# Moving one unit's input product from GpSimd to VectorE in the recurrent stage of a four-layer kernel

## The chip, the cores and the metric

The kernel runs on one core of a Trainium2 chip. A core has TensorE (matrix products, into PSUM), VectorE, ScalarE and GpSimd (elementwise work; GpSimd does not touch PSUM here), and SyncE, whose queue issues transfers. The engines run their own instruction streams and meet at semaphores. The metric is the device time of one execution in microseconds; the kernel before takes 3253.26 us (median of 3 runs, 3252.29 to 3256.7).

## The reference

Four layers one after the other on 16 sequences of 128 rows and 512 columns: an attention layer with an MLP, a grouped attention layer, a recurrent layer, and a latent attention layer with an MLP. Only the recurrent one matters here. Per sequence (l rows, h = 32 heads of s_ = 16):

```python
xm = xa[:, :, None] + sx[:, :, None] * (maa_stack + xxx)      # five mixed row sets k, w, v, r, g
w = jnp.exp(-jnp.exp(time_decay + jnp.tanh(xw @ td_w1) @ td_w2)).reshape(b, l, h, s_)
r = (xr @ Wr.T).reshape(b, l, h, s_)
k = (xk @ Wk.T).reshape(b, l, h, s_)
v = (xv @ Wv.T).reshape(b, l, h, s_)
def step(s, rkvw):
    r_t, k_t, v_t, w_t = rkvw
    a = k_t[..., :, None] * v_t[..., None, :]
    out = jnp.einsum('bhi,bhij->bhj', r_t, u * a + s)
    s = a + w_t[..., :, None] * s
    return (s, out)
```

The state s is 16 x 16 per head. The outputs are normalised per head, gated, projected and added to the input (x1); then a small gated MLP with shifted rows follows.

## The kernel before, in words

`recurrence_phase` (L2564) is the recurrent stage. A sequence's states are cut into 8 units (`UNITS`, `NU = 8`): 4 groups of 128 state rows `m` times 2 halves `jh` of the value index, in the order jh = 0 with m = 0 to 3, then jh = 1 with m = 0 to 3. The unit with index u = 4 is the fifth, (m = 0, jh = 1). Each unit has a tile of 128 x 8 x 128 values, one of four `S` buffers (`S[u % 4]`), and passes through:

1. `inputs(s, u)`: the outer product k x v for all 128 times, written to S from column 1 on. On VectorE (L3134) it reads `vb[jh]` (values copied to all partitions by SyncE's DMA, `load_v`) and the keys straight from PSUM (`k_bank`). On GpSimd (L2829) it reads `vb[jh]` and a copy of the keys in SBUF (`k_sb`), which ScalarE makes (`keys_copy`, L2988). `ON_POOL = [2, C]`, with C = 4, says which units GpSimd forms: the third and the fifth.
2. ScalarE puts the first state into column 0 (`first_states`, L2892).
3. `scan(s, u)` on VectorE (L3149): the recurrence over time, in place.
4. `multiply_states(s, u)` on GpSimd (L2818): times the receptance r, in place.
5. `sum_heads(s, u)` on TensorE (L3454): the sum over the state index, into `rec_out`. The semaphore `reduced` then frees the S buffer.

The units are interleaved by hand with the work of other sequences. `run_steps` calls each engine's `step(ahead, front, middle, back, tail)`: a step does the recurrence of one sequence (middle), the projections of the next (front), the first normalisation of the one after (ahead), the head normalisation, output projection and start of the MLP of the previous one (back), and the end of the MLP of the one before (tail). The first and last steps are written out with constants in the waits, and lack some of these parts; the steps between run in a hardware loop of two steps a turn with counts from registers.

VectorE's order in a step around the change is: `scan(middle, 3)`, `mix(front, 3)` (L3112 product, L3120 sum), `residual(back)` (L3211, which waits for the output rows `o` of TensorE, then the row statistics L3089 to L3094), `output(tail)` (L3229, L3231), `scan(middle, 4)`, `mix(front, 4)`, `stats_front(ahead)`, `inputs` and `scan` of unit 5, `inputs` of unit 6, `mix_back(back, 0)` (L3221, which waits for ScalarE's shifted rows L2940), `scan(middle, 6)`.

GpSimd's order there is: `multiply_states` of unit 3, the input product of unit 4, the back sequence's reciprocal root (`rsqrt`, L2809, L2810, L2812), `multiply_states` of unit 4, the ahead sequence's `rsqrt`, `multiply_states` of units 5 and 6.

TensorE's order there is: the transpose `rstd_t` (L3476), head sums of unit 1, the v projection, output rows 0 and 1 (L3344), head sums of unit 2, two mix products, output rows 2 and 3, and so on; the transposed back rows `normed_t` (L3331) come behind the head sums of unit 4.

The count `NA = NU - len(ON_POOL)` is the number of VectorE's input products per sequence. SyncE's `load_states` and `load_v`, and TensorE's `keys`, wait for counts of them (`a_done`).

Of the kernel before, what the change touches and what calls it, by code (L numbers as in the profile page):

```python
# [24 lines left out]
C = D // 128  # L25
# [25 lines left out]
def wait_count(engine, sem, count):  # L51

    if not isinstance(count, int) or count > 0:
        engine.wait_ge(sem, count)
# [178 lines left out]
def bcast(ap, shape, axis):  # L233
    return ap.unsqueeze(axis).to_broadcast(shape)
# [2329 lines left out]
def recurrence_phase(nc, cfg, const, x_in, x_out, ctx, state_t, weights, own_weights, next_weights):  # L2564
# [13 lines left out]
    NU = len(UNITS)  # L2578
    ROOT = 9

    ON_POOL = [2, C]
    NA = NU - len(ON_POOL)
    SETUP = 7

    with ExitStack() as stack:
        def sb(n, shape, dt=F32):
            return stack.enter_context(nc.sbuf_tensor(f"rec_{n}", shape, dt))
# [22 lines left out]
        rk = sb("rk", [128, C, T])  # L2610
        k_sb = sb("k_sb", [128, len(ON_POOL), T])
        c_sb = sb("c_sb", [128, T])
# [190 lines left out]
        def _(pool):  # L2803
# [18 lines left out]
            def inputs(s, n):  # L2822

                u = ON_POOL[n]
                m, jh = UNITS[u]
                pool.wait_ge(vb_loaded[jh], s.n * 16 + 16)
                pool.wait_ge(k_copied, s.n + 1)
                wait_count(pool, reduced, s.n * NU + u - 3)
                nc.gpsimd.tensor_tensor(S[u % 4][:, :, 1:T], vb[jh][:, :, 0:T - 1],  # L2829
                                        bcast(k_sb[:, n, 0:T - 1], [128, JH, T - 1], 1), ALU.mult)\  # L2830
                    .then_inc(pool_a_done, 1)
# [19 lines left out]
            def step(ahead, front, middle, back, tail):  # L2851
                if back:
                    multiply_states(back, NU - 1)
                if middle:
                    multiply_states(middle, 0)
                    inputs(middle, 0)
                if middle:
                    multiply_states(middle, 1)
                if back:
                    first_columns(back)  # L2860
                if middle:
                    bonus_values(middle)
                    multiply_states(middle, 2)
                if middle:
                    multiply_states(middle, 3)
                    inputs(middle, 1)
                if back:
                    rsqrt(back.n, stats2, rstd2, back_norm[2], rstd2_done)
                if middle:
                    multiply_states(middle, 4)  # L2870
                if ahead and not is_first(ahead.n):
                    rsqrt(ahead.n - 1, stats, rstd, front_norm[2], rstd_done)
                if middle:
                    multiply_states(middle, 5)
                    multiply_states(middle, 6)
# [7 lines left out]
        def _(act):  # L2883
# [99 lines left out]
            def keys_copy(s):  # L2983
                act.wait_ge(k_full, s.n + 1)
                wait_count(act, pool_a_done, s.n * len(ON_POOL))
                for n, u in enumerate(ON_POOL):
                    m = UNITS[u][0]
# [97 lines left out]
        def _(dve):  # L3085
# [42 lines left out]
            def inputs(s, u):  # L3128
                m, jh = UNITS[u]
                dve.wait_ge(vb_loaded[jh], s.n * 16 + 16)  # L3130
                if u == 0:
                    dve.wait_ge(k_full, s.n + 1)
                wait_count(dve, reduced, s.n * NU + u - 3)
                nc.vector.tensor_tensor(S[u % 4][:, :, 1:T], vb[jh][:, :, 0:T - 1],  # L3134
                                        bcast(k_bank[s.k][:, m * T:m * T + T - 1], [128, JH, T - 1], 1), ALU.mult)\
                    .then_inc(a_done, 1)

            def scan(s, u):
                m, jh = UNITS[u]
                St = S[u % 4]  # L3140
                if u in ON_POOL:
                    dve.wait_ge(pool_a_done, s.n * len(ON_POOL) + ON_POOL.index(u) + 1)
                else:
                    dve.wait_ge(a_done, s.n * NA + [v for v in range(NU) if v not in ON_POOL].index(u) + 1)
                dve.wait_ge(s0_done, s.n * NU + u + 1)
                if jh == 0:
                    dve.wait_ge(decay_done, s.n * C + m + 1)
                flat = "p j t -> p (j t)"
                nc.vector.tensor_tensor_scan(St[:, :, :].rearrange(flat), decay[m][:, :, :].rearrange(flat),  # L3149
                                             St[:, :, :].rearrange(flat), 0.0,  # L3150
                                             ALU.mult, ALU.add).then_inc(scan_done, 1)
# [82 lines left out]
            def step(ahead, front, middle, back, tail):  # L3234
                if middle:
                    inputs(middle, 0)
                    scan(middle, 0)
                if back:
                    gather(back)
                if front:  # L3240
                    mix(front, 1)
                if middle:
                    inputs(middle, 1)
                if back:
                    head_centre(back)
                if front:
                    mix(front, 2)
                if middle:
                    scan(middle, 1)
                if back:  # L3250
                    head_rsqrt(back)
                    head_norm(back)
                if middle:
                    scan(middle, 2)
                if front:
                    mix(front, 0)
                if back:
                    gated(back)
                if middle:
                    inputs(middle, 3)  # L3260
                    scan(middle, 3)
                if front:
                    mix(front, 3)
                if back:
                    residual(back)
                if tail:
                    output(tail)
                if middle:
                    scan(middle, 4)
                if front:  # L3270
                    mix(front, 4)
                if ahead and not is_first(ahead.n):
                    stats_front(ahead)
                if middle:
                    inputs(middle, 5)
                    scan(middle, 5)
                    inputs(middle, 6)
                if back:
                    mix_back(back, 0)
                if middle:  # L3280
                    scan(middle, 6)
                if back:
                    mix_back(back, 1)
                if front:
                    make_gate(front)
                if middle:
                    inputs(middle, 7)
                    scan(middle, 7)
                if ahead:
                    shift_front(ahead)  # L3290
                if front:
                    bonus_products(front)
# [552 lines left out]
```

## Time and profile before

| | value |
|---|---|
| median of 3 runs | 3253.26 us |
| profiled execution | 3253.45 us |
| its span, first to last instruction | 3251.7 us |
| TensorE busy | 3020.7 us (93%) |
| VectorE busy | 2049.7 us (63%) |
| GpSimd busy | 1259.9 us (39%) |
| ScalarE busy | 1243.0 us (38%) |
| mean granted TensorE clock | 0.976 |

The profile is of one execution. "Busy" is summed over the whole kernel, so each share is a mean over stages with different limits; the rows of the recurrent stage have to be read apart. Times in timelines are microseconds from the span's start. Releasers of waits are inferred from semaphore events.

### The profile page before, as it was taken

To read this page: it belongs to the slowest core of one execution; us is meant where nothing else is said; L and a number is where in the kernel's file an instruction comes from. 1 tells how busy PE (TensorE), PEld (TensorE's weight loads), DVE (VectorE), ACT (ScalarE), POOL (GpSimd) and SP (SyncE) were. 2 spreads that over 40 slices of the span, in tenths; PEclk is the share of its full clock that TensorE was granted. 3 is DMA by queue.
4 is the path that set the end of the run, shared out by engine and by line. 5 is a ranking of instruction groups with operands and counts; after the bars stand their busy time and mean duration, and the time that the engine had idled before them with its cause. 6 is when DMAs were issued, how large, how long until landed. Compare 5 with 4: busy or idle time off the path is not lost. (4 is left out here: it accounts for less than half of the span.)

```text
span 3251.7 us, 58799 instructions
## 1 busy us (share of the span) xinstructions
PE 3020.7 (93%) x21184; PEld 2197.2 (68%) x21184; DVE 2049.7 (63%) x3098; ACT 1243.0 (38%) x4419; POOL 1259.9 (39%) x899
## 2 busy tenths in 40 slices
PE   7999799989999889987899999997799999899999
PEld 5666566669999756655676677675455545499998
DVE  4665455564544468885899999998254454564543
ACT  2444344442322357762343443442243333332322
POOL 3555355551000045663566666666033223330000
PEclk9999899999999899998999999998899999999999
DMA  4111141110000231111111111111130011011010
GB/s 166 54 42 34 53 159 55 49 40 27 13 26 26 75 146 55 55 42 63 47 41 43 49 53 36 42 50 30 66 144 28 33 34 37 33 41 39 19 39 14
DMA packets 104318, 170.31 MB, mean 52 GB/s; under 512 B 16512, under 2 KB 54016, under 8 KB 100736
## 3 DMA queue, kind: packets, MB, share of 16 engines
q1 hardware_dynamic: 99296, 124.58, 12.0%
q10 hardware_dynamic: 4896, 44.04, 3.4%
q8 instruction: 80, 1.31, 0.2%
q14 instruction: 46, 0.38, 0.0%
HBM read 135.03 MB, written 33.55 MB: 52 GB/s over the span
## 5 line engine op out<-in xcount | busy, mean ns | idle before, releaser
L2818 POOL TENSOR_TENSOR rec_S<-rec_S,rec_r_t 128x1024 f32<-128x1024 f32 x128 | 306.1, 2392 | 255.9 <-DVE rec_S L3149 254.6
L3149 DVE TENSOR_TENSOR_SCAN rec_S<-rec_decay,rec_S 128x1024 f32<-128x1024 f32 x128 | 303.6, 2373 | 8.9 <-DVE rec_S L3134 2.1
L581 POOL TENSOR_TENSOR latent_scores<-latent_scores,region_a 128x1024 f32<-128x1024 f32 x64 | 119.9, 1895 | 390.8 <-DVE region_a L881 390.1
L1607 ACT ACTIVATE group_scores<-group_scores,group_negmax 128x128 f32<-128x128 f32 x512 | 197.6, 391 | 33.7 <-DVE group_negmax L1716 23.9
L1556 POOL TENSOR_TENSOR group_scores<-group_scores,group_rowsum 128x512 f32<-128x512 f32 x128 | 130.6, 1050 | 176.9 <-DVE group_rowsum L1730 176.9
L671 ACT ACTIVATE latent_scores<-latent_scores,region_a 128x256 f32<-128x256 f32 x256 | 126.4, 498 | 67.7 <-DVE region_a L858 67.7
L671 ACT ACTIVATE cross_scores<-cross_scores,cross_negmax 128x128 f32<-128x128 f32 x256 | 98.8, 390 | 78.0 <-DVE cross_negmax L858 77.9
L671 ACT ACTIVATE self_scores<-self_scores,self_negmax 128x128 f32<-128x128 f32 x256 | 98.7, 389 | 78.0 <-DVE self_negmax L858 77.9
L2216 ACT ACTIVATE mlp_h_t<-mlp_h_t,vectors 128x128 f32<-128x128 f32 x256 | 81.3, 390 | 114.5 <-DVE mlp_h_t L2311 92.1
L2216 ACT ACTIVATE pmlp_h_t<-pmlp_h_t,vectors 128x128 f32<-128x128 f32 x256 | 81.3, 390 | 113.5 <-DVE pmlp_h_t L2311 91.1
L3454 PE MATMUL rec_rec_out<-rec_S,head_sum 128*32 128x256 f32 x1024 | 84.1, 401 | 43.1 <-POOL rec_S L2818 42.0
L3134 DVE TENSOR_TENSOR rec_S<-rec_vb,rec_k 128x1016 f32<-128x1016 f32 x96 | 115.2, 1200 | 0.0
L1067 PE MATMUL latent_pjA<-latent_src_t,F_query_key 128*128 128x512 f32 x240 | 114.4, 600 | 0.0
L567 POOL TENSOR_TENSOR cross_scores<-cross_scores,cross_bias 128x1024 f32<-128x1024 f32 x32 | 75.1, 2358 | 77.9 <-DVE cross_scores L847 77.4
L567 POOL TENSOR_TENSOR self_scores<-self_scores,self_bias 128x1024 f32<-128x1024 f32 x32 | 75.0, 2357 | 69.3 <-DVE self_scores L847 68.8
L1607 ACT ACTIVATION_READ_ACCUMULATOR group_scores<-group_scores,group_negmax 128x1 f32 x512 | 97.9, 191 | 0.0
L868 DVE COPY region_a<-latent_pjP 128x512 f32<-128x512 f32 x48 | 32.7, 681 | 102.7 <-PE latent_pjP L1132 102.7
L581 POOL TENSOR_TENSOR cross_scores<-cross_scores,cross_rinv 128x512 f32<-128x512 f32 x64 | 68.0, 1078 | 73.0 <-DVE cross_rinv L881 73.0
L581 POOL TENSOR_TENSOR self_scores<-self_scores,self_rinv 128x512 f32<-128x512 f32 x64 | 68.0, 1079 | 72.2 <-DVE self_rinv L881 72.2
L2418 PE MATMUL pmlp_bank<-pmlp_src_t,region_a 128*128 128x128 f32 x768 | 92.7, 278 | 0.8 <-ACT pmlp_src_t L2204 0.8
L2418 PE MATMUL mlp_bank<-mlp_src_t,region_a 128*128 128x128 f32 x768 | 91.1, 275 | 1.2 <-ACT mlp_src_t L2204 1.2
L2418 PEld LDWEIGHTS pmlp_bank<-pmlp_src_t,region_a 128*128 128x128 f32 x768 | 90.5, 195 | 1.4 <-ACT pmlp_src_t L2204 1.0
(475 smaller groups left out, 7942.7 us busy)
## 6 DMA issues: line engine op xcount, KB each, us to landing
rec_vb<-v_by_head SPq DMA_DIRECT2D x32, 512.0 KB, 4.3
region_a<-in_C_w ACTq DMA_DIRECT2D x2, 4096.0 KB, 20.0
region_a<-in_G_w ACTq DMA_DIRECT2D x2, 4096.0 KB, 19.1
self_xres<-in_x SPq DMA_DIRECT2D x16, 256.0 KB, 2.7
cross_ctx_t<-in_ctx_t SPq DMA_DIRECT2D x16, 256.0 KB, 3.4
cross_xres<-rows_A SPq DMA_DIRECT2D x16, 256.0 KB, 2.6
mlp_x<-rows_B SPq DMA_DIRECT2D x16, 256.0 KB, 2.8
group_ctx_t<-in_ctx_t SPq DMA_DIRECT2D x16, 256.0 KB, 3.2
```

What stands on the lines that cost most here:

```text
L567: nc.gpsimd.tensor_tensor(half, half, bias[:, u, :].unsqueeze(1).unsqueeze(1).to_broadcast([128, 4, 2, T]), ALU.add).then_inc(bias_added, 1)
L581: nc.gpsimd.tensor_tensor(heads, heads, inverse, ALU.mult).then_inc(probs_scaled, 1)
L671: nc.scalar.activation(S[:, u, at, :], S[:, u, at, :], ACT.Exp, bias=negmax[:, u, at.start // KB:at.start // KB + 1], accum_out=rowsum[:, ...
L1067: last = nc.tensor.matmul(pj.bank(item)[:, :], Wk[:, c, n * 128:n * 128 + 128], src_t[:, c, :, :], start=c == 0, stop=c == C - 1)
L1556: nc.gpsimd.tensor_tensor(heads, heads, bcast(rowsum[:, u, 4 * r:4 * r + 4], [128, 4, T], 2), ALU.mult).then_inc(probs_scaled, 1)
L1607: nc.scalar.activation(S[:, u, at, :], S[:, u, at, :], ACT.Exp, bias=negmax[:, u, at:at + 1], accum_out=rowsum[:, u, j:j + 1])\
L2216: last = nc.scalar.activation(tile[:, n, :], tile[:, n, :], ACT.Gelu_apprx_tanh, bias=vec(cfg["b1"], half * HB + n))
L2418: last = nc.tensor.matmul(M[n][:, i * T:(i + 1) * T], w[:, c, f:f + 128], rows[:, c, :], start=c == 0, stop=c == 1)
L2818: nc.gpsimd.tensor_tensor(S[u % 4][:, :, :], S[u % 4][:, :, :], bcast(r_t[:, s.k, UNITS[u][0], :], [128, JH, T], 1), ALU.mult)\
L3134: nc.vector.tensor_tensor(S[u % 4][:, :, 1:T], vb[jh][:, :, 0:T - 1], bcast(k_bank[s.k][:, m * T:m * T + T - 1], [128, JH, T - 1], 1), ALU ...
L3149: nc.vector.tensor_tensor_scan(St[:, :, :].rearrange(flat), decay[m][:, :, :].rearrange(flat), St[:, :, :].rearrange(flat), 0.0, ALU.mult, ...
L3454: last = nc.tensor.matmul(rec_out[32 * g:32 * g + 32, jh * 2 * T:(jh + 1) * 2 * T], head_sum, S[u % 4][:, 2 * g:2 * g + 2, :], start=m == ...
```

## The change

GpSimd forms the inputs of the third unit only. VectorE forms those of the fifth too, right behind the scan of the fourth, in the S buffer that the first unit has left.

```diff
@@ -2578,7 +2578,7 @@
     NU = len(UNITS)
     ROOT = 9
 
-    ON_POOL = [2, C]
+    ON_POOL = [2]
     NA = NU - len(ON_POOL)
     SETUP = 7
 
@@ -2863,7 +2863,6 @@
                     multiply_states(middle, 2)
                 if middle:
                     multiply_states(middle, 3)
-                    inputs(middle, 1)
                 if back:
                     rsqrt(back.n, stats2, rstd2, back_norm[2], rstd2_done)
                 if middle:
@@ -3259,6 +3258,7 @@
                 if middle:
                     inputs(middle, 3)
                     scan(middle, 3)
+                    inputs(middle, 4)
                 if front:
                     mix(front, 3)
                 if back:
```

With `ON_POOL` one shorter, NA goes from 6 to 7, `keys_copy` copies one group of keys instead of two, and the waits for `pool_a_done` count one per sequence instead of two.

## Rows read from the trace of the kernel before

**Rows 1.** Stretches of the recurrent stage: us, each engine's busy time (x instructions), clock, DMA.
```profile
1523.00:2280.00 757.00, 696.08 (x5380) 508.48 (x5380) 694.38 (x922) 292.40 (x764) 486.91 (x310) 0.97 0.14 42
...
1735.63:1783.23 47.60, 45.92 (x360) 33.66 (x359) 44.43 (x61) 19.59 (x51) 30.73 (x21) 1.00 0.14 45
1783.23:1830.65 47.42, 45.51 (x356) 33.24 (x356) 44.43 (x61) 19.60 (x51) 30.57 (x21) 1.00 0.14 45
```

**Rows 2.** Timeline of TensorE: start, duration, instruction, [idle before <- releaser].
```profile
1819.79 0.33 PE L3476 MATMUL rec_bank_n<-ident,rec_hy 128*128 128x128 f32 x1 [0.46 <-DVE rec_hy L3191]
...
1828.63 1.98 PE L3344 MATMUL rec_bank_c<-region_a,rec_og_t 128*128 128x512 f32 x4
```

**Rows 3.** Timeline of VectorE in the same sequence.
```profile
1829.53 0.69 DVE L3120 TENSOR_TENSOR rec_xm<-rec_bank_b,rec_xa_t 128x512 f32<-128x512 f32 x1
1830.65 0.69 DVE L3211 TENSOR_TENSOR rec_x<-rec_bank_c,rec_xr 128x512 f32<-128x512 f32 x1 [0.43 <-PE rec_bank_c L3344]
...
1833.30 0.69 DVE L3231 SCALAR_TENSOR_TENSOR rec_y<-rec_bank_d,rec_x 128x512 f32<-128x512 f32 x1
1833.91 2.28 DVE L3149 TENSOR_TENSOR_SCAN rec_S<-rec_decay,rec_S 128x1024 f32<-128x1024 f32 x1
...
1839.91 2.29 DVE L3149 TENSOR_TENSOR_SCAN rec_S<-rec_decay,rec_S 128x1024 f32<-128x1024 f32 x1
...
1843.35 1.13 DVE L3221 SCALAR_TENSOR_TENSOR rec_f_in<-rec_bank_c,rec_w_same,rec_f_in 128x128 f32<-128x128 f32 x4
```

**Rows 4.** Timeline of ScalarE in the same sequence.
```profile
1840.44 2.88 ACT L2940 ACTIVATE rec_f_in<-rec_bank_c,vectors,rec_w_shift 128x127 f32<-128x127 f32 x8
```

**Rows 5.** Timeline of GpSimd in the same sequence.
```profile
1831.14 2.35 POOL L2829 TENSOR_TENSOR rec_S<-rec_vb,rec_k_sb 128x1016 f32<-128x1016 f32 x1
...
1834.21 1.96 POOL L2812 TENSOR_TENSOR rec_rstd<-rec_rstd 128x1 f32<-128x1 f32 x1
1836.27 2.36 POOL L2818 TENSOR_TENSOR rec_S<-rec_S,rec_r_t 128x1024 f32<-128x1024 f32 x1
...
1839.49 0.20 POOL L2812 TENSOR_TENSOR rec_rstd<-rec_rstd 128x1 f32<-128x1 f32 x1
```

**Rows 6.** The S tile's instructions: count, duration in ns (min/median/max), first and last start.
```profile
L3134 DVE TENSOR_TENSOR rec_S<-rec_vb,rec_k x96: 1181/1201/1214, 1521.9 to 2273.6; 128x1016 f32<-128x1016 f32 x96
L2829 POOL TENSOR_TENSOR rec_S<-rec_vb,rec_k_sb x32: 2343/2358/2376, 1527.8 to 2256.6; 128x1016 f32<-128x1016 f32 x32
```

**Rows 7.** Timeline of VectorE, first step (first two rows) and the loop (third).
```profile
1526.89 1.20 DVE L3134 TENSOR_TENSOR rec_S<-rec_vb,rec_k 128x1016 f32<-128x1016 f32 x1
1528.01 0.69 DVE L3112 TENSOR_TENSOR rec_bank_a<-rec_bank_a,rec_sx_t 128x512 f32<-128x512 f32 x1
...
1807.06 2.29 DVE L3149 TENSOR_TENSOR_SCAN rec_S<-rec_decay,rec_S 128x1024 f32<-128x1024 f32 x1 [0.21 <-DVE rec_S L3134]
```

**Rows 8.** Timeline of VectorE, the residual one step later.
```profile
1878.25 0.69 DVE L3211 TENSOR_TENSOR rec_x<-rec_bank_c,rec_xr 128x512 f32<-128x512 f32 x1 [0.64 <-PE rec_bank_c L3344]
```

**Rows 9.** Timeline of VectorE in the first, the second and the last step.
```profile
1545.00 0.70 DVE L3112 TENSOR_TENSOR rec_bank_b<-rec_bank_b,rec_sx_t 128x512 f32<-128x512 f32 x1 [4.96 <-PE rec_bank_b L3380]
...
1546.84 2.29 DVE L3149 TENSOR_TENSOR_SCAN rec_S<-rec_decay,rec_S 128x1024 f32<-128x1024 f32 x1 [0.34 <-POOL rec_S L2829]
...
1590.73 0.70 DVE L3112 TENSOR_TENSOR rec_bank_b<-rec_bank_b,rec_sx_t 128x512 f32<-128x512 f32 x1 [1.29 <-PE rec_bank_b L3380]
...
1606.32 1.12 DVE L3221 SCALAR_TENSOR_TENSOR rec_f_in<-rec_bank_c,rec_w_same,rec_f_in 128x128 f32<-128x128 f32 x4 [2.55 <-ACT rec_f_in L2940]
...
2254.70 0.69 DVE L3211 TENSOR_TENSOR rec_x<-rec_bank_c,rec_xr 128x512 f32<-128x512 f32 x1 [0.50 <-PE rec_bank_c L3344]
...
2258.96 2.29 DVE L3149 TENSOR_TENSOR_SCAN rec_S<-rec_decay,rec_S 128x1024 f32<-128x1024 f32 x1 [1.03 <-POOL rec_S L2829]
```

**Rows 10.** Timeline of GpSimd in the second and the last step.
```profile
1600.55 2.10 POOL L2812 TENSOR_TENSOR rec_rstd<-rec_rstd 128x1 f32<-128x1 f32 x1
...
2261.82 2.35 POOL L2818 TENSOR_TENSOR rec_S<-rec_S,rec_r_t 128x1024 f32<-128x1024 f32 x1
```

## The prediction

> **What bounds the kernel now.** I read the stretches first: the recurrent stage runs from 1523 to 2280 us, 757 us of the span [rows 1]. It handles 16 sequences; from the third on one takes 47.4 or 47.6 us in turn, with VectorE busy 44.4 us and TensorE 45.5 to 45.9 us of it, GpSimd 30.6. So two engines have little room and GpSimd has much. Which of the two sets the time changes within a sequence, and the timelines say where. From the transpose at 1819.79 TensorE runs without a gap to the output rows, whose last product starts at 1828.63 and ends at 1830.61 [rows 2]. VectorE has finished the mix for row set 3 at 1829.53 + 0.69 = 1830.22 and stands still for 0.43 us until those rows come [rows 3]. Up to there TensorE is late, by 0.43 us. From the residual (1830.65) to the scan of the fifth unit (1833.91), the sixth (1839.91), and the products at 1843.35, VectorE runs on back to back [rows 3]; ScalarE's shifted rows, ending at 1840.44 + 2.88 = 1843.32, arrive just then and themselves follow from the same fifth scan over GpSimd [rows 4]. That second half is VectorE's, and what delays the fifth scan delays the sequence.
>
> GpSimd's work on a state and VectorE's scan do not run beside each other: the last small GpSimd operation of the back sequence starts at 1834.21, inside the scan of 1833.91 to 1836.19, and lasts 1.96 us, ending at 1836.17, where it otherwise takes 0.20 [rows 5]. The input-forming product on VectorE reads one operand from PSUM, and next to a running GpSimd multiply it keeps its 1.20 us: the range over all 96 is 1181 to 1214 ns [rows 6].
>
> The Trainium skill (GPSIMD Engine Reference, Specifications) says that GpSimd shares its SBUF interfaces with VectorE and contends where VectorE's instruction has two SBUF inputs. By that the added product, with one, costs no lock, and the scans do; the rows agree.
>
> **The change, part by part.**
> *Removed on GpSimd:* 16 products of 2.36 us [rows 6], at 1831.14 in the sequence shown [rows 5]. Its end, 1833.49, lies 0.42 us before VectorE comes to the fifth scan (1833.91), so in the loop no one waits for it: worth nothing on the path. Behind it GpSimd now takes up the back sequence's root when the variance is there, about 1833.2, and ends it some 1.0 us later, ahead of the scan, rather than in it. Its reader on ScalarE is then early by nearly 2 us, but TensorE transposes those rows only behind the fifth unit's head sums, and these wait for the multiply that starts at the scan's end (1836.27, 0.08 after it) [rows 5]. No gain.
>
> *Added on VectorE:* 16 products of 1.20 us [rows 6]. What counts is what one takes from start to start of the next. Nothing in the loop shows it ahead of a mix product; in the first step such a pair starts 1.12 us apart (1526.89, 1528.01) [rows 7], and that is the lower bound. Ahead of a scan that depends on it the scan stands idle another 0.21 us (at 1807.06), which makes 1.41, the upper one [rows 7]. I take 1.15, near the like pair. Its waits are met before: the first unit's head sums, last readers of its buffer, stand in TensorE's order well ahead of the transpose of 1819.79, and the value rows of the second half and the keys are there since the step began. Queued behind it are the mix for row set 3, the residual and the output, then the fifth scan.
>
> *What idle time takes it up:* the wait for the output rows, 0.43 us in one step and 0.64 in the next [rows 3, 8]. Back-to-back starts also overlap by 0.08 (the scan at 1833.91 starts before 1833.30 + 0.69 = 1833.99) [rows 3]. Of the 13 steps whose sequence is the third to the fifteenth, 5 show 0.64 and 8 show 0.43: 6.6 us of waits, and 13 x 0.08 = 1.0 of overlap. Steps 3 to 15 cost 13 x 1.15 - 7.6 = 7.3 us, 0.6 or 0.4 us each. The next engine late there is VectorE itself.
>
> *The ends of the stage.* In the first step VectorE idles 4.96 us ahead of the mix for row set 3, so the product is free there, and the fifth scan no longer waits 0.34 us for GpSimd's input [rows 9]; with the overlap that is -0.4. In the second step it idles 1.29 us there, which hides the 1.15: 0. In the last step (no front sequence) the residual waits 0.50 us for TensorE and the fifth scan 1.03 us for GpSimd's input [rows 9]. The product takes 1.12 there (constant waits, as in the first step), of which the 0.50 and 0.08 of overlap hide a part: the residual starts 0.55 late. The fifth scan, without its 1.03 and with 0.08 of overlap, starts 1.03 + 0.08 - 0.55 = 0.56 early. Its multiply came only at 2261.82, 0.57 behind the scan's end (2258.96 + 2.29 = 2261.25), for the root in front of it ran into the scan [rows 9, 10]. That root is now done before the scan, so the multiply follows at 0.08 and gains 0.56 + 0.49, and with it the rest: -1.05.
>
> *Everything else:* the ScalarE key copy loses one of its two 0.2 us pieces and one wait; ScalarE has over 27 us idle per sequence [rows 1], so 0. The SP queue waits for the count of VectorE's products at the unit of index 3 and at the last one; both counts grow with NA and name the same instruction as before, so loads issue where they did. The second value load goes out behind the last product of the sequence before, most of a step ahead of its new first reader. If it did come late there, all of VectorE's queue would stand behind it; as GpSimd read the same buffer at 1831.14, some 2 us later than VectorE now does, with no wait before it, I cost it at nothing.
>
> *Sum:* -0.4 + 0 + 7.3 - 1.05 = +5.8 us on the profiled execution's 3253.45 (span 3251.7 and 1.75 around it; 0.2 us above the median of the runs), 3259.3. With the bounds 1.12 and 1.41 for the product: +5.5 and +9.3, 3258.9 and 3262.7. If a product costs its full 1.20 and no idle time gives way: 13 x 1.20 - 1.45 = +14.2, 3267.6.
>
> A measurement of this kernel tells a difference from none at about 0.2%, 6.5 us. The forecast lies just inside.
>
> **The rivals.**
> *A root caught by the sixth scan (slower).* For the following sequence GpSimd computes a root between the fifth multiply and the sixth scan. In the loop its last operation starts at 1839.49 and the scan at 1839.91: 0.42 us of room [rows 3, 5]. In the second step that operation started at 1600.55, inside the sixth scan, and took 2.10 us; VectorE then waited 2.55 us for ScalarE's shifted rows (1606.32) [rows 9, 10]. If the change upset the order so in every loop step, each would cost 2.5 us more: 12 x 2.5 + 5.8 = +36, 3289. It decides at a multiply more than 0.42 us late behind the fifth scan. Against it: the back root now starts 1.3 us before the scan and needs 1.0, so it frees GpSimd sooner. 0.07.
>
> *GpSimd's relief counts in each step (faster).* If the fifth scan waited for GpSimd's input in the loop too, as it does in the last step, each step would gain that 1.05: 13 x -1.05 - 1.45 = -15, 3238. Against it: the scan shows no idle ahead of it in any loop step, and 0.42 us of room. 0.08. A rule points the same way: the Trainium skill (GPSIMD Engine Reference, Engine selection) wants elementwise work on a tile on VectorE, GpSimd being about twice as slow with two inputs. The rows agree on the rate (2.36 against 1.20), and by durations alone the change would save 16 x 1.16 = 18.6 us. Rates say nothing of which engine is waited for, and here it is the one that gets the work.
>
> *The product disappears in waits (no change).* Scans behind their inputs show up to 0.21 us of idle in the loop [rows 7], and the overlaps and waits around the transposes are of the same size. If two such gaps took up another 0.4 us per step: 5.8 - 13 x 0.4 = +0.6, 3254. All of them lie in parts that move as a whole, so 0.09.
>
> *The change doesn't do what it says.* The product is issued before a mix instead of right ahead of its scan; should VectorE's own order make it wait for the head sums of the first unit, those come before the transpose of 1819.79. No separate chance.
>
> **How the numbers follow.** Forecast 0.72, of which 0.42 lies below +6.5 us and 0.30 above (the bounds +5.5 to +9.3, and unrecovered idle up to +14). Root caught 0.07, relief 0.08, no change 0.09, and 0.04 left, split evenly over slower and same. Slower 0.30 + 0.07 + 0.02 = 0.39; same 0.42 + 0.09 + 0.02 = 0.53; faster 0.08. The range goes from 3253 (the no-change case taken in) to 3267 (idle time that gives nothing); it leaves out both collisions, some 0.2 in all with the forecast's own tails. The forecast's own range is 3257 to 3263.
>
> **What would show it.** Right: VectorE has 112 products of L3134's kind and GpSimd 16; the idle of 0.43 or 0.64 ahead of the residual (L3211) is gone; the loop's sequences take about 48.0 us each, no longer in turn; the small root operation (L2812) of the back sequence lasts 0.2 and not 2 us; the fifth scan of the last sequence has no wait. Wrong if the idle is still there (then TensorE's rows moved too), if a product lasts more than 1.25 us, if L3221 shows new waits for ScalarE, or if the sequence still takes 47.5.

## The result and the profile after

The changed kernel took 3261.15 us, the kernel before 3253.74 us in runs beside it (medians of 11): a ratio of 1.0021, with a 95% interval of 1.0012 to 1.0030. That is 7.4 us more between the medians, and 3.9 to 9.8 by the interval. The forecast was 3259.3 us, +5.8. The profiled execution of after took 3259.06 us, with a span of 3257.3 us, 5.6 us longer than before's 3251.7.

First the busy times of the whole span, from the page of after, and then the stretch of the recurrent stage (columns as in [rows 1]).

```profile
PE 3018.7 (93%) x21184; PEld 2195.3 (67%) x21184; DVE 2066.4 (63%) x3114; ACT 1241.9 (38%) x4403; POOL 1197.1 (37%) x883
```
```profile
1522.50:2280.00 757.50, 694.51 (x5369) 506.81 (x5367) 710.12 (x937) 290.78 (x748) 421.20 (x291) 0.97 0.14 42
```

Against [rows 1], VectorE is busy 710.1 us where it was 694.4, GpSimd 421.2 where it was 486.9. The first difference, 15.7 us (16.7 in the totals of the two pages), is less than 16 products of 1.20 us (19.2): a product overlaps its neighbours, and busy time counts the overlap once. The second, 66 us, is more than the 16 products of 2.36 us (38 us); the rest is mostly small GpSimd operations that no longer stand in a scan. The S tile's instructions in after (count; ns min, median, max) confirm the exchange, one for one, with unchanged durations [rows 6]:

```profile
L3133 DVE TENSOR_TENSOR rec_S<-rec_vb,rec_k x112: 1178/1202/1215, 1521.1 to 2277.0; 128x1016 f32<-128x1016 f32 x112
L2829 POOL TENSOR_TENSOR rec_S<-rec_vb,rec_k_sb x16: 2340/2362/2373, 1527.1 to 2242.4; 128x1016 f32<-128x1016 f32 x16
```

The timeline of VectorE in after, one step past that of [rows 3] (a step with a wait of 0.64 before, [rows 8]):

```profile
1874.84 2.46 DVE L3148 TENSOR_TENSOR_SCAN rec_S<-rec_decay,rec_S 128x1024 f32<-128x1024 f32 x1 [0.21 <-ACT rec_S L2891]
1877.22 1.18 DVE L3133 TENSOR_TENSOR rec_S<-rec_vb,rec_k 128x1016 f32<-128x1016 f32 x1
1878.32 0.69 DVE L3111 TENSOR_TENSOR rec_bank_b<-rec_bank_b,rec_sx_t 128x512 f32<-128x512 f32 x1
1879.11 0.69 DVE L3119 TENSOR_TENSOR rec_xm<-rec_bank_b,rec_xa_t 128x512 f32<-128x512 f32 x1
1879.72 0.68 DVE L3210 TENSOR_TENSOR rec_x<-rec_bank_c,rec_xr 128x512 f32<-128x512 f32 x1
```

The added product stands between the fourth scan and the mix, and the residual behind them (L3210 now) has no wait. From the fourth scan's start to the mix's start it is 3.48 us. In before it was 2.44:

```profile
1826.29 2.46 DVE L3149 TENSOR_TENSOR_SCAN rec_S<-rec_decay,rec_S 128x1024 f32<-128x1024 f32 x1 [0.21 <-ACT rec_S L2892]
1828.73 0.70 DVE L3112 TENSOR_TENSOR rec_bank_b<-rec_bank_b,rec_sx_t 128x512 f32<-128x512 f32 x1
```

So the product adds 1.04 us to VectorE's queue, for a duration of 1.18. From its own start to the mix's it is 1.10 us (1877.22 to 1878.32), and it starts 2.38 us behind the scan, 0.06 sooner than the mix did. Behind the mix the residual now starts after 1.40 us (1878.32 to 1879.72), where it took 1.92 us in before with the wait of 0.43 and 2.13 with the wait of 0.64. So 0.52 or 0.73 us of the 1.04 are taken up there.

GpSimd in the step of [rows 5], in after:

```profile
1834.54 0.19 POOL L2812 TENSOR_TENSOR rec_rstd<-rec_rstd 128x1 f32<-128x1 f32 x1
1837.43 2.36 POOL L2818 TENSOR_TENSOR rec_S<-rec_S,rec_r_t 128x1024 f32<-128x1024 f32 x1 [2.69 <-DVE rec_S L3148]
1840.65 0.19 POOL L2812 TENSOR_TENSOR rec_rstd<-rec_rstd 128x1 f32<-128x1 f32 x1
```

The last operation of the back sequence's root ends 0.34 us before the fifth scan starts (1835.07 in after) and lasts 0.19 us, not 1.96. The following sequence's root (1840.65) is still ahead of the sixth scan (1841.06).

All marks of the stage, as a table. Each is counted from the stage's first scan, and the columns are what the kernel adds to before's mark. They are read from the timelines of VectorE.

| mark | before, us | after | after_again |
|---|---|---|---|
| residual of step 2 | 69.56 | -0.16 | -0.78 |
| residual of step 15 | 687.30 | +5.16 | +4.45 |
| last unit's head sums read | 757.32 | +4.17 | +3.80 |
| next stage's first instruction | 797.36 | +6.30 | +5.20 |

So the thirteen steps from the third to the fifteenth cost 5.3 us (5.2 in the second profile), the last step gives 1.0 (0.65) back, and the drain behind it is 2.1 (1.4) us longer, although the change touches nothing there. The stage of after begins 0.7 us earlier than before's, and 6.3 - 0.7 is the 5.6 us between the spans. In after_again the stage begins 1.65 us later than before's, so of the 7.8 us between those spans only 5.2 are the stage's own.

### The profile page after: what moved, and what is told of

It reads as the page before. It is cut to its first block and busy times, and to the rows that moved or that the text cites. A ratio compares the mean times of both kernels' runs of the same rounds, so it can differ in the third digit from the quotient of the medians.

```text
span 3257.3 us, 58793 instructions
## 1 busy us (share of the span) xinstructions
PE 3018.7 (93%) x21184; PEld 2195.3 (67%) x21184; DVE 2066.4 (63%) x3114; ACT 1241.9 (38%) x4403; POOL 1197.1 (37%) x883
## 5 line engine op out<-in xcount | busy, mean ns | idle before, releaser
L3133 DVE TENSOR_TENSOR rec_S<-rec_vb,rec_k 128x1016 f32<-128x1016 f32 x112 | 134.2, 1198 | 0.0
L2418 PEld LDWEIGHTS mlp_bank<-mlp_src_t,region_a 128*128 128x128 f32 x768 | 90.2, 194 | 1.8 <-ACT mlp_src_t L2204 1.4
```

What stands on the lines that cost most here:

```text
L2418: last = nc.tensor.matmul(M[n][:, i * T:(i + 1) * T], w[:, c, f:f + 128], rows[:, c, :], start=c == 0, stop=c == 1)
```

## Experiments

No kernel below leaves out work. Two add some: "twice" forms the fifth product two times, "idle_pool" forms it once more into a buffer that nobody reads. Ratios are to the kernel before, run beside each. A loop step is the mean of twelve, from the residual of step 3 to that of step 15; before it is 47.46 us.

**The two kernels again.** Copies of after and before, timed in the same way.

> The changed kernel once more. My theory (VectorE is the late engine from the residual to the seventh scan, and the product costs what the idle ahead of the residual does not take up): loop steps of 47.9 us on average against 47.5, no idle ahead of the residual, and 3.4 to 3.5 us lost between the first scan of the stage and the last head sums' reader, as in the first profile of it, whatever the total. The 2.1 us that the first profile lost in the drain of the stage (output rows 6.65 us against 5.36) are then the granted clock's, and may be there or not. Rival (the drain is slower because of the change): the same 2 us in the same rows again. Total 3259 to 3262 either way.

> The kernel before, once more, for a second profile. Between the reader of the last head sums and the first instruction of the next stage the profiles so far show 40.0 us (before), 42.2 and 41.4 (after), 40.5 to 41.6 (three variants). If that drain depends on the phase of the granted clock only, this one may show anything between 40 and 42; if the change makes it longer, 40.0 again. Ratio 1.000 within its interval, loop steps of 47.46 us on average.

Measured: after_again 3260.89 us, ratio 1.0020 (1.0011 to 1.0029), loop step 47.86. before_again 3254.57 us, 1.0004 (0.9995 to 1.0013), loop step 47.46 and every mark within 0.02 us of before's. The difference of 0.2% is the change's, and a mark of the loop can be read to some hundredths. Marks of the first step and of the drain can't: two profiles of the same changed kernel differ there by 0.6 and 0.7 us.

**Twice the dose.** The product is formed a second time right ahead of itself.

```diff
                     scan(middle, 3)
+                    inputs(middle, 4, True)    # counts on a semaphore of its own, and waits for it
                     inputs(middle, 4)
```

> The changed kernel with the fifth unit's product formed twice by VectorE, the second behind a wait on the first (the same values twice). My theory: the idle ahead of the residual is used up by the first, so the second costs its full 1.2 plus 0.04 to 0.2 for the wait in each of steps 3 to 15, about 1.0 in the second, nothing in the first (3.8 us of idle left), 1.2 in the last: 14 to 18 + 2 = 16 to 20 us above the changed kernel, 3277 to 3281, loop steps of 49.1 to 49.3 us. Rival (VectorE's work is hidden beside TensorE's, and the loss of the change comes from somewhere else, for instance the earlier GpSimd root or the clock): less than 5 us above the changed kernel.

Measured: 3278.21 us, 1.0074 (1.0060 to 1.0087), loop step 49.12, which is 1.67 above before and 1.26 above after. VectorE's timeline in "twice" (the two products grouped):

```profile
1836.79 2.42 DVE L3134 TENSOR_TENSOR rec_S<-rec_vb,rec_k 128x1016 f32<-128x1016 f32 x2
1839.13 0.69 DVE L3112 TENSOR_TENSOR rec_bank_b<-rec_bank_b,rec_sx_t 128x512 f32<-128x512 f32 x1
```

The pair takes 2.34 us to the mix's start. The second dose costs 1.26 us in each step, the first 0.41: the first met idle time at the residual, the second none. (The wait for its own first product is part of the 1.26.)

**The same product behind the idle time.** It is formed right ahead of the fifth scan instead of behind the fourth.

```diff
                     scan(middle, 3)
-                    inputs(middle, 4)
...
+                    inputs(middle, 4)
                     scan(middle, 4)
```

> The changed kernel with the product moved from behind the fourth scan to right ahead of the fifth, behind the residual and the output: the same VectorE work. My theory: the idle of 0.43 or 0.64 us ahead of the residual is back and absorbs nothing, and the scan that depends on the product starts 0.04 to 0.2 behind it, so each loop step costs 1.2 to 1.4 more than before the change (48.7 to 48.9 us), the whole 3271 to 3275. Rival (only VectorE's sum of work counts, not where it stands): 3261, as the changed kernel.

Measured: 3270.19 us, 1.0050 (1.0036 to 1.0064), loop step 48.78, or 1.32 above before: the step as expected, the whole 1 us under the range given. VectorE's timeline in "late", and then what the idle time ahead of its residual waited for (us, times):

```profile
1833.66 0.69 DVE L3210 TENSOR_TENSOR rec_x<-rec_bank_c,rec_xr 128x512 f32<-128x512 f32 x1 [0.43 <-PE rec_bank_c L3344]
...
1836.92 1.20 DVE L3133 TENSOR_TENSOR rec_S<-rec_vb,rec_k 128x1016 f32<-128x1016 f32 x1
1838.25 2.29 DVE L3148 TENSOR_TENSOR_SCAN rec_S<-rec_decay,rec_S 128x1024 f32<-128x1024 f32 x1
```
```profile
  PE rec_bank_c L3344: 13.1, 16
```

In after the second view reads:

```profile
  PE rec_bank_c L3344: 7.3, 2
```

Of these, one wait in either kernel is that of the drain behind the last step (5.55 us in late, 6.83 in after), and the other one in after is that of step 2 (0.42).

In late the idle time of 0.43 us is back, and the product costs its full start-to-start time, 1.33 us ahead of the scan that reads it. It is the same product at the same duration: the place makes 0.9 us per step.

**Half and three quarters of it on VectorE.** From the kernel before: GpSimd forms only the other rows, VectorE forms its part behind the fourth scan, and the fifth scan waits for both.

```diff
# GpSimd, unit 4 only: the part from j0 on
+                j0 = 0 if n == 0 else JH // 2          # three_quarters: 3 * JH // 4
# VectorE, unit 4 only: the part up to j1
+                j1 = JH // 2 if u == C else JH         # three_quarters: 3 * JH // 4
```

> The fifth unit's product cut in halves: VectorE forms rows 0 to 3 of 8 behind the fourth scan, GpSimd rows 4 to 7 in its old place. My theory: VectorE's half takes about 0.6 us, which 0.43 or 0.64 us of idle and 0.1 of overlap cover, so a loop step costs 0 to 0.1 us more than before (47.5 us) and less than half of the change's 0.4; a dose curve with its bend between half and whole. In the last step the fifth scan waits no longer for GpSimd, -1.0. Total -1.0 to +0.5 us against before. Rival (the cost is in proportion to VectorE's work): half of the change's loss, loop steps of 47.66, +2 to +3.5 us.

> The split kernel with 6 of 8 rows of the fifth product on VectorE and 2 on GpSimd. My theory (idle first, then full price): VectorE's part takes 0.25 to 0.3 us longer from start to start than the half, which left nothing of the 0.43 idle and 0.2 of the 0.64: loop steps 0.25 and 0.05 us longer than before in turn, 47.6 on average; +1 to +2 us less 1.2 in the last step, so 3252 to 3256. In proportion to the work it would be 0.3 us in every step.

Measured: split 3253.07 us, 0.9999 (0.9990 to 1.0008), loop step 47.45. three_quarters 3256.30 us, 1.0008 (0.9999 to 1.0017), loop step 47.61. VectorE's timeline in "split":

```profile
1826.28 2.45 DVE L3151 TENSOR_TENSOR_SCAN rec_S<-rec_decay,rec_S 128x1024 f32<-128x1024 f32 x1 [0.21 <-ACT rec_S L2893]
1828.65 0.65 DVE L3136 TENSOR_TENSOR rec_S<-rec_vb,rec_k 128x508 f32<-128x508 f32 x1
1829.23 0.69 DVE L3113 TENSOR_TENSOR rec_bank_b<-rec_bank_b,rec_sx_t 128x512 f32<-128x512 f32 x1
...
1830.64 0.69 DVE L3213 TENSOR_TENSOR rec_x<-rec_bank_c,rec_xr 128x512 f32<-128x512 f32 x1
```

Half a product moves the mix from 2.44 to 2.95 us behind the fourth scan, so it adds 0.51 us. The residual starts 4.36 us behind that scan, just as in before (1826.29 to 1830.65). Against VectorE's share of the product, 0, 1/2, 3/4, 1 and 2, a loop step grows by 0.00, 0.00, 0.15, 0.41 and 1.67 us. The mix comes 0, 0.51, 0.78, 1.04 and 2.28 us later. Take from this the 0.52 or 0.73 us that the place ahead of the residual can give, and the mean over the steps is the measured growth to within 0.02 us. It is flat until the idle time is full, and then it rises by the full time of the work.

**What the GpSimd relief is worth in the loop.** After, with GpSimd kept about as busy as before by a product nobody reads (two halves, 2.63 us together where one whole product took 2.36).

```diff
                     multiply_states(middle, 3)
+                    spare_product(middle)      # two halves into a buffer that is free there
```

> The changed kernel, with GpSimd still doing a product of the old size in the old place (two halves into a tile that is unused then, read by no one), so only VectorE's side of the change is there. My theory: loop steps as in the changed kernel (47.9 us), since GpSimd's relief is worth nothing there; in the last step the back root runs into the fifth scan again and the scan itself may be held, so that 1 us of the end's gain is lost: 1 to 2 us above the changed kernel, 3262 to 3263. Rival (GpSimd's relief pays in every step and hides a larger VectorE loss): 0.4 to 1 us per step more, 3267 to 3276.

Measured: 3261.34 us, 1.0022 (1.0013 to 1.0031), loop step 47.90, against 47.87 in after. GpSimd's timeline in "idle_pool":

```profile
1830.53 2.63 POOL L2838 TENSOR_TENSOR rec_xn<-rec_vb,rec_k_sb 128x508 f32<-128x508 f32 x2
1833.88 2.21 POOL L2812 TENSOR_TENSOR rec_rstd<-rec_rstd 128x1 f32<-128x1 f32 x1
```

The back root is caught by the fifth scan again (issued while the scan runs, it ends with it): 2.21 us for an operation of 0.19, and the step is 0.03 us longer. In the loop the relief is worth nothing. At the end it is worth something: from the residual of step 15 to the last head sums after gains 1.0 us on before, and idle_pool loses 0.4 (+5.74 to +6.12).

**The last step alone.** From the kernel before: only in the last sequence does VectorE form that product.

```diff
-                    inputs(middle, 1)
+                    if not is_last(middle):
+                        inputs(middle, 1)
...
                     scan(middle, 3)
+                    if is_last(middle):
+                        inputs(middle, 4)
```

> The kernel before, with the last sequence's fifth product alone on VectorE. My theory: all loop steps as before; in the last step the fifth scan starts 0.5 us earlier than before, its multiply 1.0, and the reader of the last head sums comes 1.0 us sooner: -1.0 us in the profile from the first scan to that reader, too little for the timed runs. Rival (the last step's gain in the change's profile came from the steps before): 0.

Measured: 3254.36 us, 1.0003 (0.9994 to 1.0012). The residual of step 15 is at -0.09, the last head sums at -1.16: 1.07 us gained in the last step, of which 0.39 is left at the next stage's first instruction. VectorE's timeline in "last_only" (fifth and sixth scan of the last sequence):

```profile
2259.49 2.28 DVE L3152 TENSOR_TENSOR_SCAN rec_S<-rec_decay,rec_S 128x1024 f32<-128x1024 f32 x1
2262.91 3.44 DVE L3152 TENSOR_TENSOR_SCAN rec_S<-rec_decay,rec_S 128x1024 f32<-128x1024 f32 x1
```

The fifth scan waits no longer [rows 9]. The sixth, issued while a GpSimd multiply runs, lasts 3.44 us.

**GpSimd on the sixth unit instead.** After, and GpSimd forms the sixth unit's product behind its multiply for the fourth unit, VectorE no longer. VectorE then has as many products as before, and GpSimd too. The room between the following sequence's root and the sixth scan is what is at stake.

```diff
-    ON_POOL = [2]
+    ON_POOL = [2, 5]
...
                     multiply_states(middle, 3)
+                    inputs(middle, 1)
...
-                    inputs(middle, 5)
```

> The changed kernel with the sixth unit's product given to GpSimd in return (in the place where the fifth's was), so VectorE forms six of eight again: one more in the half where TensorE is late, one less in the half where VectorE is. By VectorE's work alone: 1.2 us less per loop step than the change, 0.8 less than before, 3243 to 3246. My theory: VectorE comes to the sixth scan 1.2 us earlier, just behind the fifth multiply, and the scan catches GpSimd's small root of the following sequence, whose last operation has 0.42 us of room; ScalarE's shifted rows then come about 2 us late behind it, VectorE waits for them at the back products, and a loop step takes 48.5 to 49.5 us: 3268 to 3282.

Measured: 3287.27 us, 1.0103 (1.0088 to 1.0119), loop step 50.09. GpSimd, ScalarE and VectorE in "sixth":

```profile
1897.60 2.23 POOL L2809 TENSOR_TENSOR rec_rstd<-rec_stats,rec_single 128x1 f32<-128x1 f32 x1
1900.40 0.19 POOL L2812 TENSOR_TENSOR rec_rstd<-rec_rstd 128x1 f32<-128x1 f32 x1
```
```profile
1900.63 0.81 ACT L2924 ACTIVATE rec_x<-rec_x,rec_rstd 128x512 f32<-128x512 f32 x1 [3.14 <-POOL rec_rstd L2812]
1901.35 2.87 ACT L2940 ACTIVATE rec_f_in<-rec_bank_c,vectors,rec_w_shift 128x127 f32<-128x127 f32 x8
```
```profile
1904.26 1.12 DVE L3221 SCALAR_TENSOR_TENSOR rec_f_in<-rec_bank_c,rec_w_same,rec_f_in 128x128 f32<-128x128 f32 x4 [3.31 <-ACT rec_f_in L2940]
```

This is the slower rival of the prediction, brought about on purpose. Forming the sixth product elsewhere brings the sixth scan nearer to the root. The scan catches the root's first small operation, not its last as I had expected; ScalarE has the normalisation that needs the root in its queue ahead of the shifted rows, and VectorE waits 3.31 us for those. The price was put at 1.0 to 2.0 us per step above before and was 2.6.

**The same, with ScalarE's order changed.** The shifted rows of the back sequence come ahead of the following sequence's normalisation.

```diff
-                if ahead and not is_first(ahead.n):
-                    normalise_front(ahead)
...
                     shifted_back(back)
+                if ahead and not is_first(ahead.n):
+                    normalise_front(ahead)
```

> The kernel of the run sixth (fifth product on VectorE, sixth on GpSimd), with two entries of ScalarE's order exchanged: the shifted rows come ahead of the following sequence's normalisation, so they no longer stand behind GpSimd's caught root. If the caught root is what cost the run sixth its 2.6 us per loop step, the wait of 3.31 us ahead of the back products falls to under 1, and a step takes 47.5 to 47.9 us (the seventh scan then waits for the multiply that the root delays): 3252 to 3260. If the cost is GpSimd's and the scans' contention as such, the step stays above 49 us.

Measured: 3253.64 us, 0.9999 (0.9990 to 1.0008), loop step 47.36. GpSimd and VectorE in "sixth_act":

```profile
1832.65 2.23 POOL L2809 TENSOR_TENSOR rec_rstd<-rec_stats,rec_single 128x1 f32<-128x1 f32 x1
```
```profile
1836.88 1.13 DVE L3221 SCALAR_TENSOR_TENSOR rec_f_in<-rec_bank_c,rec_w_same,rec_f_in 128x128 f32<-128x128 f32 x4 [0.87 <-ACT rec_f_in L2940]
```

The root is caught just as before, 2.23 us, but of the wait of 3.31 only 0.87 is left. So nearly all the harm came through ScalarE's queue. A smaller one stays: the multiply for the sixth unit starts 0.70 us behind the sixth scan's end, where it is 0.08 in after, and what that costs was not tried by itself.

**Two versions built on that.** "mix_last" takes sixth_act and lets VectorE form the sixth product in the last sequence only. "mix_last_pe" also exchanges two entries of TensorE's order.

```diff
# mix_last, on sixth_act
-                    inputs(middle, 1)
+                    if not is_last(middle):
+                        inputs(middle, 1)
...
+                    if is_last(middle):
+                        inputs(middle, 5)
# mix_last_pe, on mix_last, TensorE
-                if middle:
-                    sum_heads(middle, 4)
...
                     normed_t(back)
+                if middle:
+                    sum_heads(middle, 4)
```

> The kernel of the run sixth_act, with GpSimd left out of the last sequence's sixth product (VectorE forms it there too). In sixth_act the loop steps took 47.36 us against 47.46 before, and its first steps gained 3.8 us, but the last step lost 2.0 of that, where GpSimd's input ran in front of the roots. My theory: with the last step like that of the changed kernel it gains 1 instead, so the reader of the last head sums comes some 6 us sooner than before the change, of which the clock in the drain may give back 1 to 2: 3247 to 3251, a ratio of 0.998 to 0.999. Rival (the loss of the last step has nothing to do with GpSimd's product): 3 us slower than that, as sixth_act.

> mix_last with TensorE's transpose of the back rows ahead of the fifth unit's head sums. The shifted rows then come early and VectorE's wait for them (0.87 us in sixth_act's steps) goes. My theory: nothing is won, since the seventh scan starts when GpSimd's sixth multiply lets it, at the same time as now: loop steps of 47.3 to 47.4 us. Rival (that wait is on the path): 0.5 to 0.9 us less per loop step, 3236 to 3243.

Measured: mix_last 3249.87 us, 0.9984 (0.9975 to 0.9993), loop step 47.35. mix_last_pe 3243.93 us, 0.9965 (0.9951 to 0.9978), loop step 47.26: faster than both kernels of this case. mix_last gained the 3 us expected at the last head sums (-6.10, sixth_act -3.05). For mix_last_pe I had expected next to nothing, since the seventh scan can't work before GpSimd's multiply for the sixth unit has ended. That multiply starts 11.0 us behind the residual in both kernels. GpSimd and VectorE in the loop of mix_last_pe:

```profile
1838.39 2.37 POOL L2818 TENSOR_TENSOR rec_S<-rec_S,rec_r_t 128x1024 f32<-128x1024 f32 x1
```
```profile
1838.70 1.12 DVE L3224 SCALAR_TENSOR_TENSOR rec_f_in<-rec_bank_c,rec_w_same,rec_f_in 128x128 f32<-128x128 f32 x4
1839.74 3.17 DVE L3152 TENSOR_TENSOR_SCAN rec_S<-rec_decay,rec_S 128x1024 f32<-128x1024 f32 x1
```

The wait of 0.87 ahead of the products is gone, and a scan of 2.29 us, issued 1.02 us before the multiply ends, takes 3.17 instead. That is the exchange I had reckoned with, and a step gains 0.09 us by it. What I missed is the last two steps, where VectorE waits for the shifted rows, and the seventh scan behind them lasts only 0.25 us longer without the wait. In "mix_last" it waits there:

```profile
2221.25 1.13 DVE L3224 SCALAR_TENSOR_TENSOR rec_f_in<-rec_bank_c,rec_w_same,rec_f_in 128x128 f32<-128x128 f32 x4 [0.99 <-ACT rec_f_in L2941]
...
2267.12 1.13 DVE L3224 SCALAR_TENSOR_TENSOR rec_f_in<-rec_bank_c,rec_w_same,rec_f_in 128x128 f32<-128x128 f32 x4 [1.89 <-ACT rec_f_in L2941]
```

In mix_last_pe both waits are gone, and at the last head sums it stands at -10.23, 4.1 us ahead of mix_last; 1.4 us of that was there at step 15, the rest are these two waits, nearly whole. The remaining 2.2 us of the stage come in the drain (below), and are the granted clock's.

## Why the prediction came out right, point by point

**What bounds the step.** Right, and shown. TensorE, with the output rows, was late at the residual by 0.43 or 0.64 us, VectorE everywhere behind it. "late" shows that the idle time belongs to that place, "split" that it holds half a product for nothing, "twice" that what exceeds it costs its full time.

**The added product.** The step that reasoned from the pair of the first step was right in kind and a little high: 1.15 us was taken, with 1.12 as the lower bound. From start to start it is 1.10, and the product also starts sooner behind the scan than the mix did, so it adds 1.04. With that the thirteen steps would be 13 x 1.04 - 7.6 = +5.9; measured are +5.3, predicted were +7.3. Most of the other 0.6 us stands in two places. In the third, fourteenth and fifteenth step of before the mix itself had waited 0.08 us, and there the product adds only 0.95 (3.59 us for 2.64 from scan to mix). And at the residual 8 x 0.52 + 5 x 0.73 = 7.8 us are taken up, not 7.6. That gives 10 x 1.04 + 3 x 0.95 - 7.8 = +5.4. The steps are all nearly alike now (47.93 and 47.90 in turn), as said, at 47.9 rather than 48.0.

**The first and second step.** Predicted -0.4 and 0. The second residual is 0.16 us early in one profile and 0.78 in the other. In after the first mix for row set 3 still waits 3.81 us for TensorE and the second 0.25, so the product was hidden in both, as said. Of VectorE in after:

```profile
1544.23 0.70 DVE L3111 TENSOR_TENSOR rec_bank_b<-rec_bank_b,rec_sx_t 128x512 f32<-128x512 f32 x1 [3.81 <-PE rec_bank_b L3380]
...
1589.84 0.70 DVE L3111 TENSOR_TENSOR rec_bank_b<-rec_bank_b,rec_sx_t 128x512 f32<-128x512 f32 x1 [0.25 <-PE rec_bank_b L3380]
```

**The last step.** Right in its parts. Against the mark of step 15 the residual starts 0.61 us late (0.55 was said), the fifth scan 0.50 early (0.56), and the last head sums are read 0.99 early (1.05); "last_only" gives 1.07 by itself. No new wait for ScalarE's shifted rows came up either: before the drain both kernels have three, of 2.55, 0.76 and 1.90 us. The fifth scan and the last of the three, in after:

```profile
2262.89 2.28 DVE L3148 TENSOR_TENSOR_SCAN rec_S<-rec_decay,rec_S 128x1024 f32<-128x1024 f32 x1
...
2272.76 1.13 DVE L3220 SCALAR_TENSOR_TENSOR rec_f_in<-rec_bank_c,rec_w_same,rec_f_in 128x128 f32<-128x128 f32 x4 [1.90 <-ACT rec_f_in L2939]
```

**GpSimd's relief.** Right: worth nothing in the loop ("idle_pool"), and some 1.4 us in the last step, which is that step's whole gain and more (part of it may belong to the spare product, which is 0.27 us longer than the old one). The Trainium skill (GPSIMD Engine Reference, Engine selection) speaks for the move: elementwise work belongs on VectorE, as GpSimd is about half as fast. The rate is right here too, 2.36 against 1.20 us. By these durations alone 18.6 us would be saved, and the time went the other way.

**No lock between product and GpSimd.** Right. In after the product runs at 1877.22 for 1.18 us while GpSimd's multiply runs from 1877.37 for 2.37 us, neither longer than elsewhere.

**The rivals.** The root caught by the sixth scan did not happen in after (0.41 us of room, 1840.65 to 1841.06), and it is real: "sixth" brings it about in another kernel. It takes 3287 us, where the prediction gave that rival 3289, though through another operation of the root, and at 2.2 us per step above after (50.09 for 47.86) where 2.5 was said. Relief in each step and the product vanishing in waits are both excluded by 47.87 against 47.46.

**What the sum left out.** The drain, from the last head sums to the next stage, was not in the sum and costs 2.1 us more in after and 1.4 more in after_again. That +5.8 was forecast and the profile has +5.6 is therefore luck (the medians have +7.4): 2.0 us too many for the steps and 1.4 to 2.1 us too few behind them offset each other, and the stage of after began 0.7 us early. In the drain TensorE waits for VectorE or ScalarE by turns, with three groups of its work behind the waits. They are, in before (first three lines), in after (the next three), and the third group in after_again:

```profile
2291.83 5.36 PE L3344 MATMUL rec_bank_c<-region_a,rec_og_t 128*128 128x512 f32 x8 [1.54 <-DVE rec_og_t L3203]
2301.05 0.66 PE L3331 MATMUL rec_bank_c<-ident,rec_xn 128*128 128x128 f32 x4 [3.86 <-ACT rec_xn L2924]
2305.95 5.21 PE L3338 MATMUL rec_bank_d<-rec_f_in,region_a 128*128 128x128 f32 x32 [4.24 <-DVE rec_f_in L3221]
...
2295.24 6.65 PE L3344 MATMUL rec_bank_c<-region_a,rec_og_t 128*128 128x512 f32 x8 [2.39 <-DVE rec_og_t L3202]
2305.76 1.11 PE L3331 MATMUL rec_bank_c<-ident,rec_xn 128*128 128x128 f32 x4 [3.87 <-ACT rec_xn L2923]
2311.11 5.61 PE L3338 MATMUL rec_bank_d<-rec_f_in,region_a 128*128 128x128 f32 x32 [4.24 <-DVE rec_f_in L3220]
...
2311.28 6.73 PE L3338 MATMUL rec_bank_d<-rec_f_in,region_a 128*128 128x128 f32 x32 [4.24 <-DVE rec_f_in L3220]
```

The wait of 2.39 us in after is no delay. TensorE had finished what stood ahead of it sooner, and the rows came 11.4 us behind the last head sums in both kernels. With the granted clock over each group, as a share of 2.4 GHz:

| | before | after | after_again |
|---|---|---|---|
| eight products, L3344 | 5.36 us at 0.68 | 6.65 at 0.55 | 5.12 at 0.71 |
| four transposes, L3331 | 0.66 at 1.00 | 1.11 at 0.50 | 0.66 at 1.00 |
| 32 products, L3338 | 5.21 at 0.72 | 5.61 at 0.66 | 6.73 at 0.55 |
| everything else in the drain | 28.8 | 28.8 | 28.9 |
| the drain | 40.0 | 42.2 | 41.4 |

The granted clock moves between its two levels, 1.2 and 2.4 GHz, while TensorE works and waits by turns. Each group takes longer the more of it falls into the lower level, and these three groups make up the whole difference. Over the fourteen profiles of this study the drain takes 40.0 us (before, both times, and mix_last_pe) to 42.2 (after, mix_last), with no order in what was changed, and everything but the three groups takes 28.8 to 28.9 us in all of them. So the drain's share of a difference is the clock's and not the work's. What decides at which moment the level changes stays open: no kernel here was made to try it, and two profiles of each kernel can't tell whether the change itself moves it.

## What to carry to other kernels

Before work is moved to a faster engine, find in the loop which engine is late at the place where it goes: half of this product went to VectorE for nothing, the whole cost 0.41 us of its 1.04, and the same product 5 us later in the queue cost 1.32. Price an instruction by how much later the next one starts, not by its duration. And where two engines can't run beside each other, a small operation caught by a long one cost most here (2.6 us per step) when something urgent was queued behind its reader. Changing the order of that queue took the cost away ("sixth" against "sixth_act").

## What the runs showed of the hardware

- A small GpSimd operation of 0.19 us took 1.96 to 2.23 us in the rows above when issued as a VectorE scan of 2.29 us ran, and a scan issued while a GpSimd multiply ran took 3.17 us (mix_last_pe) and 3.44 us (last_only). A product with one operand in PSUM beside the same multiply keeps its 1.18 us. The Trainium skill (GPSIMD Engine Reference, Specifications) names the shared SBUF interfaces and the case of two SBUF inputs; the rows agree, and show that the hold lasts to the end of the other's whole instruction.
- Between a scan and a mix a product of 128x1016 makes the mix start 1.04 us later and half of it 0.51, though they last 1.18 and 0.65: both are shorter in the queue than their duration by 0.14 us.
- The same drain behind the loop took 40.0 to 42.2 us by the granted clock that its matmuls met (the eight products 5.36 us at 0.68 and 6.65 at 0.55), a difference of twice what the last step gained. A sum of a few microseconds is no more certain than that.
